# A four-layer graph network on one core: the scatter adds a chunk part by part, and the near transposes and rows come later in the chunk

## The reference

```python
# L0: per-edge weights from a small MLP, summed at dst, then batch norm
w = (relu(edge_attr_16 @ W1 + b1) @ W2 + b2).reshape(E, 16, 16)
aggr = segment_sum(einsum('ei,eio->eo', x[src], w), dst)
# L1: message from x[dst] and edge_attr_8, summed at src
m = silu(einsum('ei,ej,ijh->eh', x[dst], edge_attr_8, W_msg_tp) * c) @ W_msg_lin * c2
agg = segment_sum(m, src)
# L2: two relational convolutions (l2a, l2b), mean per relation, summed at dst
# L3: degree-normalised sum of x[src] at dst
```

## Time and profile before

| | |
|---|---|
| three runs, median (lowest to highest) | 4784.44 us (4783.63 to 4788.35) |
| profiled execution, its own time | 4784.77 us |
| its span in the trace | 4783.0 us |
| busy: PE, DVE, ACT, POOL | 93%, 92%, 66%, 71% |
| matmuls L598 | 12000, 330 ns each, 2361.6 us busy |
| ACT distances L864 / one-hots L877 | 1212.7 us / 673.3 us busy |
| DVE stationary L1208 | 1500, 682 ns each, 943.4 us busy |

### The profile page before, as it was taken

One profiled execution on the slowest core, in us unless ns is written; L12 is line 12 of the kernel. 1 busy time (PEld: TensorE's weight loads), 2 busy tenths in 40 slices (PEclk: granted clock), 3 DMA queues, 4 the chain that ended last, 5 costly groups with the idle time before them and its releaser, 6 DMA issues. The chain is left out here.

```text
span 4783.0 us, 106225 instructions
## 1 busy us (share of the span) xinstructions
PE 4461.7 (93%) x29576; PEld 3064.6 (64%) x29576; DVE 4385.7 (92%) x12465; ACT 3144.2 (66%) x4959; POOL 3406.5 (71%) x2615
## 2 busy tenths in 40 slices
PE   5999999999988999999979999998999997888887
PEld 3777777777754444444437777776777775566665
DVE  5999999999988999999969999997999997999997
ACT  4777777777755666666636666665666665666665
POOL 4888888888847888888836666665666664767675
PEclk9999999999999999999989999999999998999999
DMA  2111111111112222222211111111111111111111
GB/s 68 20 18 18 18 18 18 18 18 18 18 20 64 55 56 56 56 56 57 56 35 27 27 27 27 27 25 39 26 27 26 27 27 23 28 27 28 27 28 21
DMA packets 344557, 152.04 MB, mean 32 GB/s; under 512 B 268540, under 2 KB 329032, under 8 KB 344392
## 3 DMA queue, kind: packets, MB, share of 16 engines
q0 software_dynamic: 112000, 66.23, 10.8%
q1 hardware_dynamic: 232517, 85.33, 7.3%
HBM read 138.72 MB, written 9.77 MB: 31 GB/s over the span
## 5 line engine op out<-in xcount | busy, mean ns | idle before, releaser
L598 PE MATMUL acc<-one_hot,stationary 125*128 125x392 bf16 x12000 | 2361.6, 330 | 153.2 <-ACT one_hot L877 144.6
L582 POOL DMA_INDIRECT gathered<-table_l,row_numbers x1200 | 1587.2, 1323 | 550.0 <-issue 320.8
L598 PEld LDWEIGHTS acc<-one_hot,stationary 125*128 125x128 bf16 x12000 | 1092.4, 98 | 867.0 <-issue 193.6
L864 ACT ACTIVATE distances<-count_hi,fields 125x392 bf16<-125x392 f16 (+1 forms) x2500 | 1212.7, 557 | 0.0
L849 ACT CAST mask<-is_lo 125x1024 bf16<-125x1024 f32 x500 | 521.7, 1043 | 861.4 <-DVE is_lo L1161 542.0
L582 POOL DMA_INDIRECT fields_all<-table_l,row_numbers x600 | 789.9, 1316 | 238.5 <-issue 152.7
L1208 DVE TENSOR_TENSOR stationary<-mask,parts 125x1024 bf16<-125x1024 bf16 x1500 | 943.4, 682 | 0.2 <-issue 0.2
L582 POOL DMA_INDIRECT gathered<-table_l2a,row_numbers x400 | 511.8, 1280 | 302.3 <-DVE parts L1190 136.1
L691 PE MATMUL bank<-w,h1T 128*125 128x256 f32 x3200 | 715.7, 382 | 10.0 <-DVE product L1225 8.3
L1180 DVE TENSOR_SCALAR one_hot<-count_hi,fields 125x392 bf16<-125x392 f16 x2300 | 721.1, 338 | 0.0
L755 PE MATMUL rows_ps<-node_parts,h1T 125*125 125x192 bf16 (+1 forms) x7200 | 674.1, 251 | 26.4 <-DVE node_parts L1259 19.3
(11 more groups left out here) (213 smaller groups left out, 4291.7 us busy)
## 6 DMA issues: line engine op xcount, KB each, us to landing
near_key<-near_keys_by_chunk SPq DMA_DIRECT2D x300, 122.1 KB
gathered<-table_l,row_numbers POOLq DMA_INDIRECT x1200
fields<-edge_fields SPq DMA_DIRECT2D x500, 31.2 KB
fields_all<-table_l,row_numbers POOLq DMA_INDIRECT x600
gathered<-table_l2a,row_numbers POOLq DMA_INDIRECT x400
gathered<-table_l2b,row_numbers POOLq DMA_INDIRECT x400
ea<-in_edge_attr SPq DMA_DIRECT2D x100, 62.5 KB
near_key<-near_keys_by_chunk SPq DMA_DIRECT2D x100, 61.0 KB
```

What stands on the lines that cost most here:

```text
L582: pool.indirect_dma_start(out=gathered[ph][:, s, t, :], in_=table[ph], out_offset=None, in_offset=bass.IndirectOffsetOnAxis(ap=row_numbers ...
L598: mm = pe.matmul(acc[:, :], stationary[:, s, k, t, :, :].rearrange("p a b -> p (a b)"), one_hot[:, s, t, :], start=first and t == 0 and k ...
L864: ins = act.activation(distances[:, i * n:(i + 1) * n], count_hi[:, 0:n], ACT.Abs, scale=-1.0, bias=fields[:, s, k, t:t + 1].bitcast(F32))
```

## The change

`operands` is raised by each of the three L1208 instead of by the last alone, so its values count parts: `operands_by(ph, chunk, part)` is the value at which part `part` of a chunk is there, and by default the last part. l0 and ACT's `masks` wait for the last part as before, with the new values. In the near phases PE no longer goes through the chunk tile by tile with three parts each, but part by part with eight tiles each, and waits for each part by itself. `near_turn(c+2)` stood behind 4 of 8 tiles and now stands behind hi, mid and half of low; `near_rows(c+3)` stood behind 6 of 8 tiles and now stands behind all; `near_messages(c+2)` stays last. In l1 the counts matmuls go with the hi part.

```diff
+        def operands_by(ph, chunk, part=2):
+
+            return 3 * (before(ph) + chunk) + part + 1
...
+            def add_part(ph, chunk, s, k, tiles=range(T), first=False, last=False):
+
+                for t in tiles:
+                    mm = pe.matmul(acc[:, :], stationary[:, s, k, t, :, :].rearrange("p a b -> p (a b)"), one_hot[:, s, t, :],
+                                   start=first and t == 0 and k == 0, stop=last and t == T - 1 and k == 2)
+                    if ph == "l1" and k == 0:
+                        pe.matmul(counts[0:LO, :], lo_bf[:, s, t, :], one_hot[:, s, t, :], start=first and t == 0, stop=last and t == T - 1)
+                if k == 2 and T - 1 in tiles:
+                    mm.then_inc(added, 1)
...
                 def body(chunk, pair, s):
-                    pe.wait_ge(operands, before(ph) + chunk + 1)
+                    first, last = isinstance(chunk, int) and chunk == 0, not follows(chunk, 1)
                     pe.wait_ge(scalar_hot, before(ph) + chunk + 1)
-                    add_chunk(ph, chunk, s, range(0, 4), first=isinstance(chunk, int) and chunk == 0)
+                    pe.wait_ge(operands, operands_by(ph, chunk, 0))
+                    add_part(ph, chunk, s, 0, first=first, last=last)
+                    pe.wait_ge(operands, operands_by(ph, chunk, 1))
+                    add_part(ph, chunk, s, 1)
+                    pe.wait_ge(operands, operands_by(ph, chunk, 2))
+                    add_part(ph, chunk, s, 2, range(0, 4))
                     if ph != "l3" and follows(chunk, 2):
                         near_turn(ph, chunk + 2)
-                    add_chunk(ph, chunk, s, range(4, 6))
+                    add_part(ph, chunk, s, 2, range(4, T), last=last)
                     if follows(chunk, 3):
                         near_rows(ph, chunk + 3)
-                    add_chunk(ph, chunk, s, range(6, T), last=not follows(chunk, 1))
                     if ph != "l3" and follows(chunk, 2):
                         near_messages(ph, chunk + 2, s)
...
-                    ins = dve.tensor_tensor(stationary[:, s, k], mask[:, s],
-                                            source[:, s, :, k * F:(k + 1) * F][:, :, None, :].to_broadcast([EP, T, LO, F]), ALU.mult)
-                ins.then_inc(operands, 1)
+                    dve.tensor_tensor(stationary[:, s, k], mask[:, s],
+                                      source[:, s, :, k * F:(k + 1) * F][:, :, None, :].to_broadcast([EP, T, LO, F]), ALU.mult
+                                      ).then_inc(operands, 1)
```

More of the change, by code:

```diff
@@ L702, in l0 @@
                 if later(chunk, 2):
-                    pe.wait_ge(operands, before("l0") + chunk - 1)
+                    pe.wait_ge(operands, operands_by("l0", chunk - 2))
                     pe.wait_ge(scalar_hot, before("l0") + chunk - 1)
@@ L724, in l0 @@
                     for n in (CHUNKS - 2, CHUNKS - 1):
-                        pe.wait_ge(operands, before("l0") + n + 1)
+                        pe.wait_ge(operands, operands_by("l0", n))
                         pe.wait_ge(scalar_hot, before("l0") + n + 1)
@@ L842, in masks @@
                 if later(chunk, 2):
-                    act.wait_ge(operands, before(ph) + chunk - 1)
+                    act.wait_ge(operands, operands_by(ph, chunk - 2))
                 if ph == "l1":
```

## The result

The changed kernel takes 5182.46 us (median of 4 runs, 5176.33 to 5189.74), the kernel before 4786.40 us beside it (4783.63 to 4791.78): a ratio of 1.0829, 95% interval 1.0813 to 1.0845. It is 396 us slower. The forecast was slower by 183 us, with a range that ended at 5011 us. The profiled execution has 5177.99 us and a span of 5176.2 us.

A forecast was written before the change was run, and what follows sets the result against it. The prediction took DVE to set the pace, 9.73 us a chunk in l1. It summed 4784.8 + 114 (late turn) + 69 (clock falls in half of l1's chunks) = 4968 us, with a range of 4882 to 5011 us.

The forecast's parts named there:

- The part waits: PE's waits in l1 and l3: the one-hots come last, so waiting part by part gains nothing.
- The turn and the circle: l1: turn starts 6.15 us into PE's chunk, was 3.43; 10.89 us round against DVE's 9.73, costing 114 us.
- the circle: l1: PE's chunk, near turn, ACT's copy, one-hots, PE's next chunk; 8.17 us before, 10.89 us after.
- The clock in l1: PE's pauses drop its clock to 1.2 GHz in half of l1's chunks, 1.4 us each: 69 us.
- the new pause: PE's standing time before each next l1 chunk in the changed kernel, put at 1.5 to 1.7 us.
- the rival of a fall in each chunk: PE's clock falls in every l1 chunk, adding 137 us instead of 69: 5036 us; chance 0.05.
- a clock that holds: Rival: PE's clock doesn't fall in l1, so only the 114 us are added: 4899 us; chance 0.29.
- the rival of the hidden circle: l1: acc and counts pairs cost at most 0.33 us, DVE's 9.73 stays the pace: 4785 us; chance 0.05.
- l2a and l2b: Turn 1.33 us later, within its slack, and rows 1.0 us later: nothing, upper bound 24 us.
- The rows: Near rows in l2a and l2b 1.0 us later, 0.12 us too late for DVE: nothing, upper bound 24 us.
- a sign of being wrong: Prediction is wrong if DVE waits for L755 (near rows) in l2 and l3, or L977 isn't idle in l1.
- l3: Rows 1.0 us later, mostly taken in by PE's pauses: nothing, upper bound 19 us.

The follow-up runs named there:

- e5: The changed kernel with one wait of PE a chunk, for the low part, instead of three; 5180.23 us.
- e3: The changed kernel with ten more matmuls of zeros into acc behind the messages of each l1 chunk, filling PE's pause; 4935.17 us.
- e8: The changed kernel with ACT's copy of the near turn behind the chunk's one-hots in l1, PE's order untouched; 4876.59 us.
- e4: The changed kernel with l1's near turn behind hi and four tiles of mid; 4822.69 us.
- e10: The changed kernel with l1's eight counts matmuls moved out of the hi part, in a row behind the near turn; 4816.30 us.
- e2: The kernel before, tile by tile, with l1's near turn behind 7 of 8 tiles and its rows behind all tiles; 4948.58 us.
- e7: The changed kernel with l1's eight counts matmuls in a row behind the hi part's acc matmuls; 4875.26 us.
- e1: The changed kernel with l1's near turn right behind the hi part; 4831.65 us.
- e6: The kernel before with only the near rows moved, behind all eight tiles in every near phase; 4826.31 us.

## Why the prediction was wrong

**The part waits: right.** "No gain", and e5 shows no cost either. The one-hots still come last, at 2025.15 where the parts are ready at 2024.65.

**The turn and the circle: right in place and size.** Pairs were to cost 0.52: the changed kernel's first one takes 0.52, those of e3 0.53. The turn was to start at 6.15 us with the clock held: 6.25 in e3. Copy 0.48 later: 0.42. From the copy to PE's next start 4.26: 4.25. With 6.15 + 0.42 + 4.25 = 10.82, the circle alone costs 98 x (10.82 - 9.73) = 107 us where 114 were forecast. e3, the one run with that circle and a clock that held, was 152 us over before; part of the difference is its later copy in every second chunk. The waits that were to show it are there, on L995 from PE's turn and on L1208 from ACT's silu, in 97 and 98 chunks. e8, which takes the one-hots out of the circle, and e4 and e10, which make the turn earlier, each give most of the loss back.

**The clock in l1: this is the step that failed.** It said: "I take a fall in half of the chunks, 49 x 1.4 = 69 us", with an upper bound of 137 us for a fall in each. Both factors were too small. The clock falls in practically every chunk, and a fall delays the turn by 8.94 - 6.15 = 2.79 us, not 1.4. That makes 98 x 2.79 = 273 us; e3 against the changed kernel measures it as 247. With 107 of the circle, 8 of l2 and 3 ahead of l1 it is 391 us; the two profiled executions are 5177.99 - 4784.77 = 393 apart.

The number of falls was set from two pauses, 1.43 us without a fall in l3 and 1.73 us with one, and the new pause was taken to lie between. It came out at 1.75 to 1.84 us, above the row that showed a fall. The sum had it at 1.5 to 1.7, since it put PE's way from the turn's start to its last message at 3.1 to 3.3 us; that takes 2.92 (2020.61 to 2023.53). e3 shows that the pause is what brings the falls in this order: filled, there are none.

The length of a fall was read from one chunk in the order of before, where it is 3.3 us. That row holds for that order: e2, which keeps it, has 3.4 us again, and e7 with rows of acc and of counts has 3.4 us. With pairs of acc and counts behind the fall it is 6.7 to 6.8 us, in the changed kernel and in e8. So the rival of a fall in each chunk, which had a chance of 0.05, had the number of falls right and was still 146 us short; its 5036 us was no bound, since it priced the new order by a row of the old one. The falls of e1, with pairs, last 6.7 us too, and those of e10, without pairs, 3.4. Why PE gets the clock back later behind pairs was not settled; the runs show only which order goes with which length.

The Trainium skill (TensorE: Matmul & The Clock Gate, "Why this matters for your kernels") warns of longer pauses than those here, and the prediction weighed that as a reason for a clock that holds. The rows here differ: 1.84 and 1.75 us ahead of chunks in which the clock fell to 0.50. Another section of that page of the Trainium skill, "A second HAM failure mode: psum-queue depth-cycling", tells of a clock that goes up and down where PE idles shortly between groups of matmuls, again and again; that is what l1 shows, 0.50 for half of its time, and the prediction didn't weigh it. The rule of the Trainium skill on weight loads pulled ahead (the same page, "Part 2: What happens when you issue a matmul") stood behind the rival of the hidden circle. Matmuls 0.165 apart would fit it; the counts of e7 in a row come near that, 0.18 us each, and the pairs, 0.52 to 0.53, do not.

**l2a and l2b: small, but not nothing.** The rows were set at nothing with an upper bound of 24 us. DVE does wait for them now, 27.5 us in 93 chunks of l2a, which the prediction named as a sign of being wrong, and the two phases are 8 us longer. Alone, in e6, the same lateness costs some 28 us in l2 and 15 us in l1. The first is over the bound of 24 us, and for the second the prediction had no term.

**l3: right.** 695 us hold the same work at a clock of 1.00.

## What to carry to other kernels

The place of a step that another engine waits for begins to matter where the circle through it passes the pace of the engine that bounds. Count the circle with all that the new order puts ahead of the step (here eight acc and four counts matmuls more), for below that point the place is nearly free and beyond it each chunk pays. When the bound leaves an engine and PE begins to stand a little in each chunk, price the clock as part of the circle: a fall delays the step that the others wait for, and its length should come from a run with the new order of matmuls, not from a row of the old one. If no such run exists, the upper end of the range has to lie well above one fall in each chunk at the old length.

## What the runs showed of the hardware

- In the stretches shown the clock stayed at 1.2 GHz for 3.4 us in the orders of e2, e7 and e10, and for 6.7 to 6.8 us where pairs of acc and counts followed, in the changed kernel, e1 and e8.
- The length of a pause didn't decide by itself whether the clock fell: 1.75 us was followed by a fall and 1.99 us by none in e7, 2.72 us by none in e10, and 1.04 us by a fall in e1.
- A counts matmul costs 0.18 us in a row of its own kind (e7), and as much as 0.26 to 0.27 between acc matmuls (e3: 2010.87, 2011.13, 2011.40). The list of waits puts 242.8 us on 785 of the counts' weight loads in the changed kernel. The kernel before has that as well, in l1, 1460 to 2425, so it is no part of the loss:

```profile
PEld counts L605 <- issue: 258.0, 793, 0.6
```

- Ten more matmuls a chunk made the kernel 247 us faster (e3 against the changed one): with them the clock was 1.00 in the stretch of l1, without them 0.75.
